# Score products on two row tiles, and score broadcasts on two column tiles, in the tail of a vision-tower kernel

## The reference

```python
h = concat([cls_tok, h])                      # (32, 65, 64)
# attention: 8 heads of width 8, window of 32 tokens to each side
qkv = layernorm(h) @ w_qkv + b_qkv
scores = einsum('bld,blwd->blw', q, k_w) / sqrt(8)      # per image and head
attn = softmax(scores);  out = einsum('blw,blwd->bld', attn, v_w)
h = h + out @ w_proj + b_proj
# ffn: 64 experts, the best 6 per token
x = layernorm(h)
logits = x @ gate_w.T;  top, idx = top_k(logits, 6);  s = softmax(top)
xW = einsum('bsd,bskde->bske', x, W[idx]);  y = einsum('bske,bsk->bse', xW, s)
out = layernorm(x + y @ out_w.T + out_b) * ln_g + ln_b;  h = h + out
```

## Time and profile before

| | |
|---|---|
| median of 3 runs | 1089.97 us (1087.08 to 1090.45) |
| the profiled execution, its own time | 1089.02 us |
| its span (first to last instruction) | 1086.0 us |
| outside the span | 3.0 us |
| Fourier network | 0 to 808 us of the span |
| queries, keys, values | 808 to 834 us |
| attention | 834 to about 932 us |
| experts, first broadcast to last product | 953.8 to 1075 us |
| mean granted TensorE clock | 0.979 of 2.4 GHz |

### The profile page before, as it was taken

The page is one execution under the profiler, slowest core; times in us unless marked ns, Lnnn a source line. Parts: engine busy times, 40 slices in busy tenths (PEclk is TensorE's granted clock), DMA queues, the critical chain, the costliest instruction groups (busy, mean ns, idle before and its releaser), DMA issues.

```text
span 1086.0 us, 36279 instructions
## 1 busy us (share of the span) xinstructions
PE 996.6 (92%) x16844; PEld 620.2 (57%) x16844; DVE 618.7 (57%) x773; ACT 410.1 (38%) x554; POOL 155.2 (14%) x159
## 2 busy tenths in 40 slices
PE   4899899999989998999999899999999999589996
PEld 3567567656657533676576567656126888522221
DVE  2278357637734222576378358542254677779887
ACT  2332233323223495332232233324767787321100
POOL 6000000000000000000000000120011764234411
PEclk9999999999999899999999999999899999689999
DMA  5220230031023102300320220020010000000000
GB/s 194 93 78 3 78 94 2 5 116 54 3 93 121 36 6 73 85 20 4 105 66 3 94 77 3 17 94 2 13 21 36 2 1 1 2 1 1 1 10 10
DMA packets 25916, 46.71 MB, mean 43 GB/s; under 512 B 9949, under 2 KB 11000, under 8 KB 25125
## 3 DMA queue, kind: packets, MB, share of 16 engines
q1 hardware_dynamic: 24118, 42.47, 12.7%
q0 software_dynamic: 1456, 1.60, 0.5%
q10 hardware_dynamic: 192, 0.33, 0.1%
HBM read 30.21 MB, written 10.89 MB: 38 GB/s over the span
## 4 chain that ended last, share of the span: by engine, by line
PE 75%; DVE 12%; issue 6%; ACT 4%; POOL 2%; DMA 1%; SPq 0%; POOLq 0%; DVEq 0%
PE PSALL L1298 22%; PE PSALL L1266 7%; PE PSALL L1160 5%; PE PSALL L1289 5%; PE PSALL L1375 5%; PE PSALL L1241 4%; PE PSALL L1174 4%; PE PSALL L526 3%; PE PSALL L1385 3%; DVE WORK L1505 3%; PE PSALL L429 3%; DVE WORK L1524 2%; DVE WORK L1005 2%; PE PSALL L514 2%; PE PSALL L1285 2%
## 5 line engine op out<-in xcount | busy, mean ns | idle before, releaser
L1524 DVE STREAM_TRANSPOSE WORK<-PSALL 128x1024 f32<-128x1024 f32 x128 | 152.4, 1229 | 249.6 <-PE PSALL L1266 249.6
L1298 PEld LDWEIGHTS PSALL<-EW,WORK 128*64 128x64 f32 x4096 | 221.8, 138 | 72.7 <-issue 48.3
L1298 PE MATMUL PSALL<-EW,WORK 128*64 128x128 f32 x4096 | 247.6, 276 | 14.0 <-DVE WORK L1524 13.7
L1424 ACT ACTIVATE X<-PSALL,TABLES 128x1024 f32<-128x1024 f32 x128 | 141.9, 1115 | 306.7 <-PE PSALL L1298 306.7
L1505 DVE STREAM_TRANSPOSE WORK<-PSALL 128x1024 f32<-128x1024 f32 x84 | 104.3, 1241 | 32.7 <-PE PSALL L1160 30.9
L325 POOL DMA_DIRECT2D WORK<-MIXED x32 | 17.9, 560 | 667.1 <-ACT MIXED L1415 553.8
L1406 ACT COPY SPEC<-PSALL 128x400 f32<-128x400 f32 x64 | 53.8, 850 | 135.7 <-PE PSALL L1174 132.8
L1174 PEld LDWEIGHTS PSALL<-TABLES,WORK 128*64 128x64 f32 x2000 | 67.0, 138 | 48.9 <-DVE WORK L1505 31.4
L1005 DVE TENSOR_TENSOR WORK<-PSALL,X 128x832 f32<-128x832 f32 x80 | 79.7, 1018 | 19.2 <-PE PSALL L514 18.0
L1174 PE MATMUL PSALL<-TABLES,WORK 128*64 128x64 f32 x2000 | 80.7, 228 | 8.0 <-DVE WORK L1505 3.8
L1458 ACT ACTIVATE WORK<-PSALL,B 128x1024 f32<-128x1024 f32 x64 | 68.0, 1111 | 20.9 <-PE PSALL L1375 20.6
(11 more groups left out here) (158 smaller groups left out, 1154.7 us busy)
## 6 DMA issues: line engine op xcount, KB each, us to landing
SW<-in_spec_w SPq DMA_DIRECT2D x160, 80.0 KB, 2.7
spec_scr<-MIXED SPq DMA_DIRECT2D x24, 400.0 KB, 3.3
SPEC<-spec_scr SPq DMA_DIRECT2D x32, 200.0 KB
WORK<-spec_scr SPq DMA_DIRECT2D x16, 200.0 KB
WORK<-in_coords_w SPq DMA_DIRECT2D x2, 1024.0 KB, 4.9
XC<-in_coords_c SPq DMA_DIRECT2D x2, 1024.0 KB, 7.2
WORK<-MIXED SPq DMA_DIRECT2D x40, 40.0 KB
WORK<-MIXED POOLq DMA_DIRECT2D x32, 40.0 KB
```

Source lines behind the costliest of these rows:

```text
L1298: m = pe.matmul(PS[2 * p + z][64 * j:64 * j + 64, 2 * b * GRID:(2 * b + 2) * GRID], G[:, n % 2, b, h:h + 2, :, t].rearrange("p q o -> p (q ...
L1424: nc.scalar.activation(X[:, n].rearrange("p b (z d) c w -> p d z b (c w)", z=2)[:, p, :, :, 2 * t * GRID:2 * (t + 1) * GRID], PSALL[:, 2 * ...
L1524: nc.vector.transpose(G[:, n % 2, 2 * x + y].rearrange("p h o v -> p o h v"), PSALL[:, 4 + 2 * x:6 + 2 * x, :].rearrange("p k (h o v) -> p ...
```

## The change

It does five things.

1. **Queries and keys are held twice.** The weights of queries and of keys stand twice side by side (`WQKV` grows from 192 to 320 columns), so that the same two matmuls (L357, L360) give queries and keys on partitions 0 to 63 and again on 64 to 127. ACT's copies (L590, L593) write 128 partitions in place of 64.
2. **Masks for two heads in one instruction.** `HM` has the masks of heads 0 to 3 on its upper and those of heads 4 to 7 on its lower 64 partitions. `mask_keys` (L575) is one instruction on 128 partitions where it was two on 64.
3. **Scores on two row tiles.** The first matmul of an image uses rows 0 to 63 of the array (heads 0 to 3), the second rows 64 to 127 (heads 4 to 7), 64 rows each.
4. **Broadcasts on two column tiles.** Each broadcast is two matmuls with 64 weight columns each, on the two column tiles that the expert products use.
5. **What goes with it.** POOL no longer clears the lower keys (`KMZ`), and the wait for that goes. The memory that the wider tensors take is found by halving the buffer for POOL's DMA descriptors (4096 to 2048).

```diff
-        WQKVZ, WP = sb("WQKV", [128, 3 * GRID]), sb("WP", [GRID, GRID])
+        WQKVZ, WP = sb("WQKV", [128, 5 * GRID]), sb("WP", [GRID, GRID])
-        HM = sb("HM", [GRID, HEADS])
+        HM = sb("HM", [128, HEADS // 2])
...
-                pe.matmul(PS[3][:, 0:CT], WQKVZ[:, GRID:3 * GRID], x, start=True, stop=True).then_inc(k_full, 1)
+                pe.matmul(PS[3][:, 0:CT], WQKVZ[:, 2 * GRID:4 * GRID], x, start=True, stop=True).then_inc(k_full, 1)
...
-                    pe.wait_ge(km_ready, HEADS * (b // BC + 1))
+                    pe.wait_ge(km_ready, HEADS // 2 * (b // BC + 1))
                 if b == 0:
-                    pe.wait_ge(keys_zeroed, 1)
                     pe.wait_ge(probs_zeroed, 1)
...
-                    m = pe.matmul(SPR[b % 2][:, hf, :], QTW[:, b * TOK:b * TOK + 128],
-                                  KMZ[:, b // BC % 2, 4 * hf:4 * hf + 4, b % BC * TOK:(b % BC + 1) * TOK],
-                                  start=True, stop=True)
+                    m = pe.matmul(SPR[b % 2][:, hf, :], QTW[64 * hf:64 * hf + 64, b * TOK:b * TOK + 128],
+                                  KM[64 * hf:64 * hf + 64, b // BC % 2, :, b % BC * TOK:(b % BC + 1) * TOK],
+                                  start=True, stop=True, tile_position=(64 * hf, 0))
...
-                m = pe.matmul(PS[n % 4][:, 0:ZT], SEL[:, ep % (EH // 2), :], PARTS3[:, 2 * ep // EH, z * ZT:(z + 1) * ZT],
-                              start=True, stop=True)
+                for i in range(2):
+                    m = pe.matmul(PS[n % 4][64 * i:64 * i + 64, 0:ZT], SEL[:, ep % (EH // 2), 64 * i:64 * i + 64],
+                                  PARTS3[:, 2 * ep // EH, z * ZT:(z + 1) * ZT],
+                                  start=True, stop=True, skip_group_check=True, tile_position=(0, 64 * i))
...
-                nc.scalar.activation(QT[:, c * CT:(c + 1) * CT], PS[2][0:GRID, 0:CT], ACT.Identity, bias=BQK[:, 0:1]
+                nc.scalar.activation(QT[:, c * CT:(c + 1) * CT], PS[2][:, 0:CT], ACT.Identity, bias=BQK[:, 0:1]
...
-                    mask_keys(c + 1, range(2 * r, 2 * r + 2))
+                    mask_keys(c + 1, r)
...
-            nc.gpsimd.memset(KMZ[GRID:128], 0.0).then_inc(keys_zeroed, 1)
-            pool.wait_ge(keys_zeroed, 1)
...
-    nc = bacc.Bacc("TRN2", target_bir_lowering=False, num_devices=1, dynamic_dma_scratch_size=4096)
+    nc = bacc.Bacc("TRN2", target_bir_lowering=False, num_devices=1, dynamic_dma_scratch_size=2048)
```

More of the change, by code:

```diff
@@ L243, in vit_kernel @@
         QTW = arena[:, 10272:10272 + NT + 128]
-        QT = QTW[0:GRID, 0:NT]
-        KT = arena[0:GRID, 12352:12352 + NT]
+        QT = QTW[:, 0:NT]
+        KT = arena[:, 12352:12352 + NT]
         V = T1[0:TOK, 0].rearrange("p a b -> p (a b)")[:, 0:NIMG * HEADS * VH].rearrange("p (b h e) -> p b h e", b=NIMG, h=HEADS)
@@ L251, in vit_kernel @@
         sw_mem = SW[:].rearrange("p a b c -> p (a b c)")
-        KMZ = sw_mem[:, 8320:8320 + 2 * HEADS * CT].rearrange("p (r h t) -> p r h t", r=2, h=HEADS)
-        KM = KMZ[0:GRID]
+        KM = sw_mem[:, 8320:8320 + HEADS * CT].rearrange("p (r h t) -> p r h t", r=2, h=HEADS // 2)
         HT = HEADS * TOK
@@ L365, in qkv @@
                     m = pe.matmul(PS[4][0:TOK, i * GRID:(i + 1) * GRID], YT[0:GRID, b * TOK:(b + 1) * TOK],
-                                  WQKV[:, 2 * GRID:3 * GRID], start=True, stop=True)
+                                  WQKV[:, 4 * GRID:5 * GRID], start=True, stop=True)
                 m.then_inc(v_full, 1)
@@ L571, in deviation, with mask_keys @@
                 nc.scalar.activation(st[:, 2, a], st[:, 1, a], ACT.Sqrt).then_inc(dev_ready, 1)
-            def mask_keys(c, heads):
-                for h in heads:
-                    nc.scalar.activation(KM[:, c % 2, h, :], KT[:, c * CT:(c + 1) * CT], ACT.Copy,
-                                         scale=HM[:, h:h + 1]).then_inc(km_ready, 1)
+            def mask_keys(c, h):
+                nc.scalar.activation(KM[:, c % 2, h, :], KT[:, c * CT:(c + 1) * CT], ACT.Copy,
+                                     scale=HM[:, h:h + 1]).then_inc(km_ready, 1)
             for k in range(LK - 1):
@@ L585, in tail_scalar @@
                 if c >= 4:
-                    mask_keys(0, range(2 * (c - 4), 2 * (c - 3)))
+                    mask_keys(0, c - 4)
                 if c + 1 < NC:
@@ L589, in tail_scalar @@
                 act.wait_ge(q_full, c + 1)
-                nc.scalar.activation(QT[:, c * CT:(c + 1) * CT], PS[2][0:GRID, 0:CT], ACT.Identity, bias=BQK[:, 0:1]
+                nc.scalar.activation(QT[:, c * CT:(c + 1) * CT], PS[2][:, 0:CT], ACT.Identity, bias=BQK[:, 0:1]
                                      ).then_inc(q_ready, 1)
                 act.wait_ge(k_full, c + 1)
-                nc.scalar.activation(KT[:, c * CT:(c + 1) * CT], PS[3][0:GRID, 0:CT], ACT.Identity, bias=BQK[:, 1:2]
+                nc.scalar.activation(KT[:, c * CT:(c + 1) * CT], PS[3][:, 0:CT], ACT.Identity, bias=BQK[:, 1:2]
                                      ).then_inc(k_ready, 1)
@@ L610, in gate_logits_out @@
                 if c == 0:
-                    act.wait_ge(km_ready, HEADS * NC)
+                    act.wait_ge(km_ready, HEADS // 2 * NC)
                 nc.scalar.copy(LG[:, c * BC:(c + 1) * BC, 0:EXPERTS],
@@ L1689, in layout @@
     ffn = {k[len("L0_ffn_"):]: v for k, v in a.items() if k.startswith("L0_ffn_")}
-    d["w_qkv"], d["w_proj"] = att["w_qkv"], att["w_proj"]
-    d["b_qk"] = att["b_qkv"][0:2 * GRID].reshape(2, GRID).T
+    wq, wk, wv = np.split(att["w_qkv"], 3, axis=1)
+    d["w_qkv"], d["w_proj"] = np.concatenate([wq, wq, wk, wk, wv], 1), att["w_proj"]
+    d["b_qk"] = np.tile(att["b_qkv"][0:2 * GRID].reshape(2, GRID).T, (2, 1))
     every = lambda v: np.tile(v, (TOK, 1))
```

6 lines of the change are left out of this document (3 added, 3 removed).

## The result

The changed kernel takes 1082.54 us (median of 12 runs, 1076.1 to 1086.36), the kernel before 1089.75 us (12 runs beside them, 1087.08 to 1091.76). The ratio is 0.9938 with a 95% interval of 0.992 to 0.9956: faster by 0.6%, 6.8 us by the ratio and 7.2 us between the medians. Forecast were 1081 us and a range of 1072.5 to 1087.5. A second measurement of the same kernel gave 1083.87 us and 0.9945 (0.9926 to 0.9963).

What follows compares the result with a forecast made beforehand. PE was taken to bound attention, with PE and DVE close in the expert loop. Attention steps 4.9, start of attention 1.0 and experts 2.7 make 8.6 us off 1089.02: 1080.4, stated as 1081, range 1072.5 to 1087.5.

Steps and rivals of the forecast that it cites:

- Scores in a plain step: Attention steps not behind a projection or logits: scores on PE go from 0.93 to 0.78 us, saving 0.15 a step.
- Behind projections: Seven attention steps behind a projection or the gate's logits: tile changes stay at two, so 0.45 us is saved each.
- 80% arrives: Attention steps 5 to 31: of 6.2 us saved on PE, 80% shortens the time, 4.9 us; bounds 50% (3.1) and 100%.
- The start of attention: Up to step 4's scores: 0.7 us from shorter first scores, 0.3 from halved masks, 1.0 in all; bounds 0.3 and 1.2.
- rival 3: Attention, 889 to 918 us: halved score work makes PE seem idle, its granted clock falls, 1094 us; chance 0.05.
- Experts: Expert loop: broadcasts on two column tiles cut a PE step from 1.31 to 1.04 us, saving 2.7 in all; bounds 1 and 6.
- Masks, copies, clearing, buffer at 0: Halved masks outside attention's start, copies on 128 partitions, POOL's dropped clearing and the smaller descriptor buffer: 0 us each.
- The whole half arrives: Attention and experts: weight loads and drains are hidden, 18.5 us saved, 1071 us; chance 0.14.
- tiles don't run side by side: Scores or broadcasts: one of the two tiled forms doesn't run side by side, slower at 1094 us; chance 0.04.
- Turned into a wait: Attention and experts: faster PE then waits for ACT's copy and DVE's side jobs, 2.7 us saved, 1087 us; chance 0.12.
- The clock falls: Another name for rival 3: PE's granted clock falls in attention at 889 to 918 us, 1094 us; chance 0.05.

Runs made afterwards that it cites:

- changed again: The changed kernel, unedited, measured a second time on the same chip: 1083.9 us, ratio 0.9945 to the kernel before.
- scores alone: The changed kernel with broadcasts as before (one matmul of 128 weight columns), the rest of the change kept: 1083.7 us, ratio 0.9961 to the kernel before.
- masks twice: The changed kernel with each of the 32 masks issued twice to the same place, ACT waiting between the two: 1084.6 us, ratio 0.9947 to the kernel before.
- more extra matmuls: The changed kernel with 4, 2, 2, 2, 3 and 1 unused matmuls ahead of the scores of steps 0 to 5: 1082.4 us, ratio 0.9928.
- extra matmuls: The changed kernel with 1, 1, 1 and 3 unused matmuls ahead of the scores of steps 1 to 4: 1078.3 us, and 1083.3 when run again.
- one score product: The changed kernel with only the first of an image's two score products (heads 4 to 7 left out): median 1113.4 us, range 1083.9 to 1127.9.
- experiments 4 and 5: The changed kernel with only the first score product of each image (4: 1113.4 us), and with only the first 64 columns of each broadcast (5: 1080.5 us).
- half broadcasts: The changed kernel with only the first 64 columns of each broadcast: 1080.5 us, ratio 0.9919 to the kernel before.

## Why the prediction was right, and where it was not

**Scores in a plain step**, forecast at 0.78 us: right, as a sum. The group itself is 0.64, with 0.10 on the values ahead and 0.05 on the transposes behind. The step went from 2.40 to 2.26, a saving of 0.14 for 0.15. The price of the tile change was read in the expert loop, and it held in attention. The Trainium skill (TensorEngine Tiling (Array Packing), Key Properties) says that a change of tiling mode drains the engine; the trace agrees, with 0.10 + 0.18 + 0.05 = 0.33 us for two changes and the longer weight loads in attention, and 0.26 for two in the expert loop.

**Behind projections**, forecast at 0.45 saved: a little less. L440 and the scores take 0.41 + 0.70 us for 0.61 + 0.99, less 0.10 on the values and 0.05 on the transposes, 0.34. On DVE, images 10 and 18 follow the one before after 2.73 us instead of 3.16, 0.43 less. It can't be read at each such step: images 14, 22 and 30 follow 0.12 to 0.13 us later than before, and the ones behind them 0.64, 0.53 and 0.14 sooner.

**80% arrives**: right. From image 8 to 31, 23 steps, the terms of the prediction make 7 x 0.45 + 16 x 0.15 = 5.55, of which 80% is 4.44 us. Measured were 66.30 - 61.82 = 4.48. The lost fifth is where the prediction put it: in this stretch PE's wait for ACT's copy rose from 2.0 to 3.6 us, and DVE's lumps didn't move (image 24 follows 23 after 3.96 us in both kernels, 16 follows 15 after 3.36 and 3.35). The share itself was a guess, and luck has a part in how well it fits: in the second profile the stretch takes 61.21 us, 5.09 won or 92%.

**The start of attention is the step that failed**, in the images behind step 4. Forecast were 1.0 us won up to the scores of step 4 and 0.5 in steps 5 to 8 (four plain steps at 80%). The first came: 7.63 us from the first scores to step 4's, then 6.63. The terms in it were close. The first score brought 0.94 for 0.7, but 0.5 of that is the clock, which happened to be up there (1.16 us to image 0 in the kernel before when it is); in three profiles with the new scores in which it fell as before (changed again, scores alone, masks twice), it brought 0.63 to 0.76. The masks brought 0.41 for 0.3 (two in a row took 0.90 us, one of 128 partitions takes 0.49), and the subtraction on POOL started 1.91 us behind DVE's first product instead of 1.56, which took 0.35 away. From image 4 to image 8, however, 10.29 us became 12.09, and 14.71 in the second profile: 1.8 and 4.4 lost where 0.5 was forecast to be won. What decides there is the clock. The prediction's sum had the clock of these steps at 1.00, as before. Its rival 3 had the mechanism, with a chance of 0.05, but looked for it from 889 us on; with less work in a thin stretch the clock fell at 842.7 us, and the steps that are PE's bound ran at 1.2 GHz. It is also what the prediction itself named as a sign of being wrong: a granted clock under 1.0 between 844 and 918 us. With the clock up (more extra matmuls), images 4 to 8 take 10.07 for 10.29, and 9.40 where the fall is over before image 4 (extra matmuls). The Trainium skill (TensorE: Matmul & The Clock Gate, The HAM clock gate) says that the clock follows how busy PE has been; the run with one score product shows the clock at 0.50 for 45 us with PE's records at 44.45 us busy, so in this kernel the busy time that the profile shows doesn't tell it.

**Experts**, forecast at 2.7 us: 3.0. The step on PE is 1.05 for 1.04, the run of steps without a wait went as said, rows and projections stayed (1.79 for 1.82), and DVE's waits for broadcasts fell by 2.7 us in all. The small rest: the steps between projections are 1.27 for 1.31.

**Masks, copies, clearing, buffer at 0**: nothing in the runs speaks against it. The copies on 128 partitions, of which the prediction had no row, take 473 ns in the mean (L590), and 473 before on 64; the masks 509 for 504.

**Rivals.** *The whole half arrives* fell with the 2.26 us step, *tiles don't run side by side* with experiments 4 and 5. *Turned into a wait* holds for a fifth. *The clock falls* came true in small, at another place.

**The number.** From the first scores to the end, the forecast was 8.6 us less; the two profiles of the changed kernel have 6.6 and 4.7 less. In the first one, the 3.1 us between its 1083.5 and the sum's 1080.4 are mainly 2.3 from images 4 to 8 and 2.2 from the later start of attention, against 0.3 more from the experts and 1.1 less outside the span. That the median came within 1.5 us of the forecast is partly luck.

**The spread** can't be put down to the fall in attention. Among the 12 runs of the changed kernel, six have a mean granted clock of 0.978 to 0.981 and took 1076.1 to 1081.6 us, six have 0.972 to 0.974 and took 1083.5 to 1086.4. But the profiled execution with half broadcasts has 0.978 and 1080.4 us, and its attention is that of the changed kernel's first profile (0.973, 1083.5 us) to 0.02 us, with the same fall. Of the 3.0 us between their spans, 2.9 lie ahead of the first scores (833.83 against 836.76), in the Fourier network, where the clock was lower for 6.8 us in one and for 17.1 us in the other. And the kernel before has the same spread, 1083.1 to 1092.9 us in 23 runs at mean clocks of 0.974 to 0.983.

What stays open: what exactly makes the clock fall in one execution and not in the next, in attention and in the Fourier network, and where the quickest runs (1076.1 to 1077.1 us) kept it, since none of them was profiled. No version here is measurably quicker than the changed kernel for holding it up.

## What to carry to other kernels

Price a tile change by a place in the same trace where two tiles alternate; here a pair of changes cost 0.26 to 0.33 us, and it made a halved 0.93 us group worth 0.14 in one place and 0.34 in the other, while putting neighbours on one tile shape paid the full 0.26. When PE gets less to do, look first at the thinnest stretch ahead of the place where PE is the bound: the clock that falls there is paid for in the steps behind it. And when single runs lie in two groups, compare profiles of both groups from a common point on before giving the difference to a stretch, and repeat the measurement before choosing a version.

## What the runs showed of the hardware that was not expected

- Leaving out one of two products that run side by side on row tiles left the scores group at 0.63 us, and made the kernel 30 us slower in the median: the granted clock was 0.50 to 0.56 from 844 to 920 us, with PE busy nearly all the time.
- Two 64-column bf16 matmuls of 416 columns side by side take 0.17 us, as one of them does, and as one of 128 columns takes by the columns alone.
- Extra matmuls that keep PE busy (1.07 us for two, in steps of 1.33) brought nothing measurable: 1083.3 (one a step) and 1082.4 us (two a step) against 1083.9.
